# Splitting the first queries' transfer, and reordering the prologue of a one-core attention and expert layer

## Chip, cores and metric

One core of a Trainium2 chip runs one program. The metric is device time in microseconds of one execution; less is better. Times within a trace count from the first instruction.

## What is computed

A transformer layer on x of 2 x 1024 x 128 float32, with 16 heads of 8 columns that share one key and one value head, causal attention, and a routed feed-forward part:

```python
mod = (_silu(L0_c) @ L0_wmod).reshape(L0_c.shape[0], 6, 1, -1)
sa, ca, ga, sb, cb, gb = (mod[:, i] for i in range(6))   # ga, gb: sign kept, magnitude at least 0.25
h = _layernorm(x, axis=-1) * (1 + ca) + sa
x = x + ga * attn(h, w_attn, w_proj)     # q: 16 heads of 8; k, v: one head of 8; softmax over k <= q
h = _layernorm(x, axis=-1) * (1 + cb) + sb
x = x + gb * ffn(h, ...)                 # top 4 of 16 experts by sigmoid gate, plus a shared expert
```

## The kernel before

**Tiling.** The 2048 tokens are 16 units u of 128 tokens and 4 chunks of 512. Chunks are taken in the order `CHUNKS` = 0, 2, 1, 3; c0 is chunk 0 (units 0 to 3 of batch 0), c1 is chunk 2 (units 8 to 11, the start of batch 1). For a unit, two things run on TensorE over its keys: first the maxima (`max` jobs: scores with queries as columns, reduced by VectorE at L768 to one maximum per query and head, 4 jobs for unit 0, 8 for unit 1, 16 for unit 2), then, with the maximum added as two more contraction rows, the `scores` blocks (exponentiated by ScalarE, L628) and the products with the values (`pv`). The maximum of a unit is split into two bfloat16 parts, transposed (`shift`), copied by ScalarE and sent by a transfer into rows 96 and 97 of `qa` (L426).

**Queries and keys.** float32 products are made from bfloat16 parts: a query is split into three parts `qp[0]`, `qp[1]`, `qp[2]` (ScalarE L600, then `q_rest` on VectorE or GpSimd), and six copies of them are stacked in 48 rows of `qa`. `qp` has (feature, head) on its 128 partitions, `qa` has 8 features x 6 products on partitions and heads along the row, so the stacking is six transfers for each chunk (L409), each from 128 partitions of `qp` into 8 partitions of `qa`. Rows 48 to 95 of `qa` are mask marks, sent by `mark` (L376); those of `ka` come once, from `k_marks` (L395). A key chunk is made by `k`, `k_rest`, `k_mid`, `k_set`; a value chunk by `v`. `hT` is the normalized, modulated, transposed input of a chunk, made from `xn` (`norm`), whose statistics are `stats`.

**Order.** One list, `plan`, is written before the program, and every engine walks it in order and does its part of each entry, with semaphores between. The prologue is written out by hand. The rest is made by a loop over the attention blocks: four `scores` steps to a block, each followed by `step`, which advances a clock `now` by 0.87 and emits what is due: maxima by their due steps, and the entries of `side` and `smalls` (each with the time from which it may be emitted). So an entry in `side` with time 2.0 is emitted at the third step. Block n is written scores(n, g), g = 0 to 3. The blocks of unit 0 are n = 0, of unit 1 n = 1, 2, of unit 2 n = 3 to 5, of unit 3 n = 6 to 9.

**Queues.** All transfers that the change touches are issued by SyncE (SP), in the order of the plan, into one queue; SP goes to the next entry as soon as the waits of its own part are met. `fetch` are the expert weights' loads (six issues, L416 to L421). TensorE's `warm` entries are products of the identity with itself whose result nobody reads. The small PSUM bank of `hT`, `k` and later entries is free for the next user when the last one's reader has read it (`small_free`).

Of the kernel before, what the change touches and what calls it, by code (L numbers as in the profile page):

```python
# [5 lines left out]
def adaln_attention_moe_kernel(nc, x_d, w_attn_d, w_proj_d, gate_d, ws_in_d, vs_in_d, ws_out_d,  # L6
# [7 lines left out]
    HD = (w_attn_d.shape[1] - D) // 2  # L14
# [5 lines left out]
    CH = 4 * P  # L20
# [16 lines left out]
    PRODUCTS = ((0, 2), (0, 1), (1, 1), (0, 0), (1, 0), (2, 0))  # L37
# [11 lines left out]
    LAST = CHUNKS[-1]  # L49
# [6 lines left out]
    jobs = []  # L56
    for u in order:
# [4 lines left out]
        w = (t + 1) * P - k0  # L62
# [85 lines left out]
    def one_max():  # L148
        j = st["job"]
        st["job"] += 1  # L150
        plan.append(("max", j))
        if j == last_job[jobs[j][0]]:
            emit(("split_max", jobs[j][0]))
# [26 lines left out]
    def step(cost):  # L180
# [5 lines left out]
    plan += [("stats", c0), ("silu",), ("norm", c0), ("warm", 11), ("cond",), ("warm", 2), ("stats", c1), ("norm", c1)]  # L186
    plan += [("hT", c0), ("warm", 3), ("q", c0), ("q_rest", c0)]
    plan += [("k", c0), ("k_rest", c0), ("k_mid", c0), ("v", c0), ("k_set", c0)]
    side += [(3.0, ("k_set", c1)), (4.0, ("stats", CHUNKS[2])), (6.0, ("stats", CHUNKS[3]))]
    smalls += [(5.0, ("gates",))]  # L190
    side += [(8.0, ("norm", CHUNKS[2])), (90.0, ("norm", CHUNKS[3])), (1.0, ("marks",)), (2.0, ("fetch",)), (20.0, ("w_split", 0)),
             (24.0, ("w_split", 1)), (27.0, ("w_split", 2)), (10.0, ("sentinels",))]

    def through_shift(u):
        while st["job"] <= last_job[u]:
            one_max()
        while ("shift", u) not in plan:
            x = next(x for x in smalls if x[1] == ("shift", u))
            smalls.remove(x)
            emit(x[1])  # L200
# [2 lines left out]
        while st["job"] <= last_job[u]:  # L203
            one_max()

    plan += [("hT", c1), ("q", c1), ("q_rest", c1)]
    max_of(order[0])
    plan += [("k", c1), ("k_rest", c1)]
    max_of(order[1])
    through_shift(order[0])  # L210
    plan += [("k_mid", c1), ("v", c1)]
    for j in range(4):
        one_max()
    through_shift(order[1])
    for n, (u, kt, first, last) in enumerate(blocks):
        if first:
            through_shift(u)
# [57 lines left out]
    with ctx:  # L275
# [3 lines left out]
        def sem(name):  # L279
            return ctx.enter_context(nc.semaphore(name))  # L280
# [65 lines left out]
        x_in = [sem(f"x_in{c}") for c in range(NC)]  # L346
        w_attn_in, w_proj_in, c_in, wmod_in, gate_in = (sem("w_attn_in"), sem("w_proj_in"), sem("c_in"), sem("wmod_in"),
                                                        sem("gate_in"))
        q_in = [sem(f"q_in{c}") for c in range(NC)]
        shift_in = [sem(f"shift_in{u}") for u in range(NU)]  # L350
        consts, wk_ready, rows_ready, cleared = sem("consts"), sem("wk_ready"), sem("rows_ready"), sem("cleared")
# [30 lines left out]
        @block.sync  # L382
        def _(sp):
            xv = x_d.rearrange("b (t p) d -> p (b t) d", p=P)
            sp.dma_start(xs[:, 4 * c0:4 * c0 + 4, :], xv[:, 4 * c0:4 * c0 + 4, :]).then_inc(x_in[c0], 16)
            sp.dma_start(w_attn[:, :], w_attn_d).then_inc(w_attn_in, 16)
            for c in CHUNKS[1:]:
                sp.dma_start(xs[:, 4 * c:4 * c + 4, :], xv[:, 4 * c:4 * c + 4, :]).then_inc(x_in[c], 16)
            sp.dma_start(gate_w[:, :], gate_d).then_inc(gate_in, 16)
            sp.dma_start(w_proj[:, :], w_proj_d).then_inc(w_proj_in, 16)  # L390
            sp.wait_ge(q_marked, 1)
            mark(sp, c0)
            sp.wait_ge(k_marked, 1)
            for b in range(B):
                sp.dma_start(ka[QROWS:QROWS + 64, 1, b, :].rearrange("p (t k) -> p t k", k=P),  # L395
                             k_marks[QROWS:QROWS + 64, :].unsqueeze(1).broadcast_to([64, TB, P])
                             ).then_inc(k_marks_in, 16)
            for x in plan:
                kind = x[0]
                if kind == "q_rest":  # L400
                    c = x[1]
                    b, t0 = c // CB, c % CB * CH
                    sp.wait_ge(q_hi, q_no[c] + 1)
                    for i in range(3):
                        if i == 1:
                            sp.wait_ge(q_parts, q_no[c] + 1)
                        for n in range(len(PRODUCTS)):
                            if PRODUCTS[n][0] == i:
                                sp.dma_start(qa[HD * n:HD * (n + 1), b, :, t0:t0 + CH],  # L409
                                             qp[i][:, q_no[c] % 2, :]).then_inc(q_in[c], 16)  # L410
                elif kind == "marks":
                    for c in CHUNKS[1:]:
                        mark(sp, c)
                elif kind == "fetch":
                    for i, w_d in enumerate((e_win_d, e_vin_d)):
                        sp.dma_start(sl[:, 2 * i:2 * i + 2, :].rearrange("p s (e f) -> p (s e) f", f=F),  # L416
                                     w_d.rearrange("e d f -> d e f")).then_inc(w_in, 16)
                    sp.dma_start(w_out[:, 1:, :], e_wout_d.rearrange("(c s) f d -> (s f) c d", s=EC)).then_inc(w_in, 16)
                    sp.dma_start(sl[:, 4, 0:P], ws_in_d).then_inc(w_in, 16)
                    sp.dma_start(sl[:, 4, P:2 * P], vs_in_d).then_inc(w_in, 16)  # L420
                    sp.dma_start(w_out[:, 0, :], ws_out_d).then_inc(w_in, 16)  # L421
                elif kind == "shift":
                    u = x[1]
                    b, t = u // TB, u % TB
                    sp.wait_ge(small_read[at[x]], use[x] + 1)
                    sp.dma_start(qa[MROWS:SROWS, b, :, t * P:(t + 1) * P], shiftT[:, place[u] % 2, :]  # L426
                                 ).then_inc(shift_in[u], 16)
                elif kind == "combT" and x[1] != LAST:
                    c = x[1]
                    sp.wait_ge(small_read[at[x]], use[x] + 1)  # L430
                    sp.dma_start(comb_d[c], combT[:, :]).then_inc(comb_out[c], 16)
                elif kind == "spread":
                    c = x[1]
                    sp.wait_ge(comb_out[c], 16)
                    if turn_of[c]:
                        sp.wait_ge(gated_up, FC * turn_of[c])
                    rows = comb_d[c].rearrange("(f s) t -> s f t", s=EC)
                    for s in range(EC):
                        sp.dma_start(comb_wide[F * s:F * s + F, :, :],
                                     rows[s].unsqueeze(0).broadcast_to([F, FC, CH])).then_inc(comb_in[c], 16)  # L440
                elif kind == "turn":
                    c = x[1]
                    ov = out_d.rearrange("b (t p) d -> p (b t) d", p=P)
                    sp.wait_ge(small_read[at[x]], use[x] + 1)
                    sp.dma_start(ov[:, 4 * c:4 * c + 4, :], xs[:, 4 * c:4 * c + 4, :]).then_inc(out_sent[c], 16)
            for c in range(NC):
                sp.wait_ge(out_sent[c], 16)

        @block.gpsimd
        def _(gp):  # L450
# [33 lines left out]
            for x in plan:  # L484
                kind = x[0]
                if kind in ("norm", "norm2"):
# [6 lines left out]
                    own(gp.tensor_scalar(rstd[:, us], mv[:, us, 1], EPS, None, ALU.add))  # L493
                    gp.tensor_tensor(rstd[:, us], rstd[:, us], neg_half[:, :], ALU.pow).then_inc(rstd_ready, 1)  # L494
                    k = norm_no[x]
                    if x not in (("norm", c0), ("norm2", LAST)):
                        gp.wait_ge(rstd_ready, k + 1)
                        if k >= 2:
                            before = xn_of[norms[k - 2]]
                            gp.wait_ge(small_ready[at[before]], use[before] + 1)  # L500
                        for i in range(4):
                            u = 4 * c + i
                            ins = gp.tensor_scalar(xn[:, k % 2, i, :], xs[:, u, :], mv[:, u, 0:1], rstd[:, u:u + 1],  # L503
                                                   ALU.subtract, ALU.mult)
                        ins.then_inc(xn_ready, 1)
# [69 lines left out]
        def _(act):  # L575
            act.dma_start(cT[:, :], c_d.rearrange("b d -> d b"), allow_slow_non_contiguous=True).then_inc(c_in, 16)
            act.dma_start(wmod[:, :, :], wmod_d.rearrange("k (j d) -> k j d", j=6)).then_inc(wmod_in, 16)
            for x in plan:
# [15 lines left out]
                elif kind == "q":  # L594
# [2 lines left out]
                    act.wait_ge(small_ready[at[x]], use[x] + 1)  # L597
                    if k >= 2:
                        act.wait_ge(q_in[CHUNKS[k - 2]], len(PRODUCTS) * 16)
                    act.activation(qp[0][:, k % 2, :], small[at[x]][:, :], ACT.Copy).then_inc(q_hi, 1)  # L600
                elif kind == "k":
                    c = x[1]
# [64 lines left out]
        def _(v):  # L667
# [7 lines left out]
            for x in plan:  # L675
                kind = x[0]
                if kind == "stats":
# [6 lines left out]
                    for u in range(4 * c, 4 * c + 4):  # L684
                        ins = v.bn_aggr(mv[:, u, :], stat6[:, u, :])
                    ins.then_inc(stats_ready, 1)
                elif x in (("norm", c0), ("norm2", LAST)):
                    c, k = x[1], norm_no[x]
                    if k >= 2:
                        before = xn_of[norms[k - 2]]  # L690
# [157 lines left out]
        def _(pe):  # L848
# [9 lines left out]
            for x in plan:  # L858
# [43 lines left out]
                elif kind == "max":  # L902
# [3 lines left out]
                    if x[1] == 0 or jobs[x[1] - 1][0] // 4 != u // 4:  # L906
                        pe.wait_ge(k_marks_in, 16 * B)
                        pe.wait_ge(q_marks_in[u // 4], 16)
                        pe.wait_ge(q_in[u // 4], len(PRODUCTS) * 16)
                        pe.wait_ge(k_done, q_no[u // 4] + 1)  # L910
                    if k >= NM:
                        pe.wait_ge(m_read, k - NM + 1)
                    to = m_bank[k % NM][:, 0:n * w].rearrange("p (n w) -> p n w", w=w)
# [143 lines left out]
```

## Time and profile before

| | us |
|---|---|
| median of 3 executions | 440.38 |
| lowest, highest | 437.97, 493.62 |
| the profiled execution | 439.45 |
| its span, first to last instruction | 436.9 |
| TensorE busy in the span | 381.4 |
| VectorE busy | 271.5 |
| ScalarE busy | 222.2 |
| GpSimd busy | 97.0 |

The span is that of the profiled execution; 2.55 us of its time lie around it. Engines are named PE (TensorE), PEld (its weight loads), DVE (VectorE), ACT (ScalarE), POOL (GpSimd), SPq (SyncE issuing transfers). A busy share is an average over stages, so what matters here is read from the first 80 us. TensorE's granted clock has two levels, 1.00 (2.4 GHz) and 0.50 (1.2 GHz); a mean between them is a stretch with both. The share of DMA is that of 16 engines.

### The profile page before, as it was taken

What the parts mean: (1) busy time and instruction counts of PE and PEld (TensorE: products, weight loads), DVE (VectorE), ACT (ScalarE), POOL (GpSimd) and SP (SyncE); (2) the same over time, 40 slices, a digit from 0 to 9 for tenths busy, and PEclk for the clock granted to TensorE, in tenths of its full rate; (3) what the DMA queues carried; (4) which work ended last, traced back from release to release, by engine and by line L of the source; (5) the groups of instructions that cost most, each with busy time, mean ns of one, the idle gap of its engine ahead of it and who ended that gap; (6) DMA issues with size and microseconds to landing.
All of it is one profiled execution on the core that took longest, in us unless ns stands there. A gap on an engine that the chain in (4) does not pass through costs nothing.

```text
span 436.9 us, 5857 instructions
## 1 busy us (share of the span) xinstructions
PE 381.4 (87%) x2065; PEld 178.4 (41%) x2065; DVE 271.5 (62%) x624; ACT 222.2 (51%) x413; POOL 97.0 (22%) x128
## 2 busy tenths in 40 slices
PE   8449879899999986999899999987999998848995
PEld 7235433443463442443554334342534333216542
DVE  4429974898986956794468747865278734113343
ACT  2301437656668642463675545763875446834300
POOL 6511095302300393310260000050046000011000
PEclk9755889999999996999999999996999999995999
DMA  8653951400005300418100000000530000000000
GB/s 209 85 62 49 231 135 27 49 2 2 2 1 137 61 2 0 53 21 173 23 24 3 1 0 26 1 2 0 128 71 2 1 0 26 0 2 0 1 0 24
DMA packets 21851, 17.84 MB, mean 41 GB/s; under 512 B 6656, under 2 KB 18576, under 8 KB 21824
## 3 DMA queue, kind: packets, MB, share of 16 engines
q1 hardware_dynamic: 21408, 17.09, 20.6%
q10 hardware_dynamic: 416, 0.39, 0.3%
q8 instruction: 16, 0.26, 0.3%
q14 instruction: 11, 0.09, 0.1%
HBM read 9.65 MB, written 1.15 MB: 25 GB/s over the span
## 4 chain that ended last, share of the span: by engine, by line
PE 66%; DVE 15%; ACT 6%; POOL 4%; issue 4%; DMA 3%; SPq 1%; POOLq 0%; ACTq 0%; DVEq 0%
PE bank L850 62%; DVE mn L768 9%; DMA qa<-qp 3%; ACT pr L628 2%; POOL xn L503 2%; PE bank L997 2%; POOL rstd L494 1%; ACT L628 1%; PE bank L883 1%; POOL sl L572 1%; SPq L409 1%; ACT fT L663 1%; DVE stat L800 1%; ACT osb L640 1%; ACT hT L592 1%
## 5 line engine op out<-in xcount | busy, mean ns | idle before, releaser
L768 DVE TENSOR_REDUCE mn<-bank 128x1 f32<-128x512 f32 (+3 forms) x304 | 186.5, 655 | 72.6 <-PE bank L850 72.0
L628 ACT ACTIVATE pr<-bank 128x512 f32<-128x512 f32 x288 | 159.3, 598 | 100.2 <-PE bank L850 98.6
L850 PE MATMUL bank<-ka,qa 96*128 96x128 bf16 (+3 forms) x576 | 113.8, 291 | 19.2 <-DVE mn L768 9.8
L850 PE MATMUL bank<-qa,ka 98*128 98x512 bf16 x288 | 109.8, 392 | 4.2 <-DMA qa<-shiftT 2.3
L850 PE MATMUL bank<-pr,va 128*32 128x512 f32 x576 | 80.2, 630 | 0.7 <-ACT pr L628 0.7
L850 PEld LDWEIGHTS bank<-ka,qa 96*128 96x128 bf16 x576 | 51.3, 104 | 68.7 <-DVE mn L768 27.9
L850 PE MATMUL bank<-hT_parts,up_parts 128*128 128x512 f32 x216 | 66.2, 439 | 1.2 <-DVE sl L840 1.1
L850 PEld LDWEIGHTS bank<-qa,ka 98*128 98x128 bf16 x288 | 28.1, 100 | 88.4 <-ACT pr L628 47.7
L850 PEld LDWEIGHTS bank<-hT_parts,up_parts 128*128 128x128 f32 x216 | 40.9, 200 | 18.6 <-issue 6.3
L572 POOL TENSOR_TENSOR sl<-sl,comb_wide 128x512 f32<-128x512 f32 x24 | 29.9, 1278 | 55.1 <-DMA comb_wide<-comb_rows 27.7
L840 DVE TENSOR_TENSOR sl<-sl,bank 128x512 f32<-128x512 f32 x36 | 24.7, 687 | 24.6 <-PE bank L850 19.7
L493 POOL TENSOR_SCALAR rstd<-mv 128x4 f32<-128x4 f32 x8 | 1.9, 233 | 167.9 <-DVE mv L801 167.7
L850 PE MATMUL bank<-sl,w_out 128*128 128x512 f32 x72 | 37.3, 599 | 0.0
L632 ACT ACTIVATE sl<-bank 128x512 f32<-128x512 f32 x36 | 21.4, 599 | 7.8 <-PE bank L850 6.2
L850 PEld LDWEIGHTS bank<-pr,va 128*32 128x32 f32 x576 | 11.5, 109 | 21.6 <-ACT pr L628 11.4
L503 POOL TENSOR_SCALAR xn<-xs,mv,rstd 128x128 f32<-128x128 f32 x24 | 19.4, 820 | 0.6
L640 ACT ACTIVATE osb<-bank 128x512 f32<-128x512 f32 x16 | 9.6, 597 | 16.2 <-PE bank L850 16.2
L592 ACT ACTIVATE hT<-bank,mod 128x512 f32<-128x512 f32 x8 | 6.2, 777 | 22.7 <-PE bank L883 22.7
L789 DVE RECIPROCAL rec<-bank 128x16 f32<-128x16 f32 x16 | 4.0, 252 | 20.0 <-PE bank L997 19.9
L997 PE MATMUL bank<-ident,osb 128*128 128x128 f32 x64 | 9.9, 277 | 6.6 <-ACT fT L663 3.8
L850 PEld LDWEIGHTS bank<-sl,w_out 128*128 128x128 f32 x72 | 13.0, 190 | 4.7 <-DVE sl L840 0.8
L663 ACT ACTIVATE fT<-bank,gs 128x512 f32<-128x512 f32 x4 | 2.8, 688 | 22.9 <-PE bank L850 22.9
(128 smaller groups left out, 257.8 us busy)
## 6 DMA issues: line engine op xcount, KB each, us to landing
comb_wide<-comb_rows SPq DMA_DIRECT2D x6, 1024.0 KB, 9.9
qa<-q_marks SPq DMA_DIRECT2D x4, 768.0 KB, 8.8
qa<-qp SPq DMA_DIRECT2D x24, 128.0 KB
xs<-in_L_attn_x SPq DMA_DIRECT2D x4, 256.0 KB, 5.3
out_x<-xs SPq DMA_DIRECT2D x4, 256.0 KB, 2.3
sl<-in_L_ffn_e_win SPq DMA_DIRECT2D x1, 512.0 KB, 11.0
sl<-in_L_ffn_e_vin SPq DMA_DIRECT2D x1, 512.0 KB, 10.6
w_out<-in_L_ffn_e_wout SPq DMA_DIRECT2D x1, 512.0 KB, 5.1
```

The costliest lines, as they stand in the source:

```text
L409: sp.dma_start(qa[HD * n:HD * (n + 1), b, :, t0:t0 + CH], qp[i][:, q_no[c] % 2, :]).then_inc(q_in[c], 16)
L503: ins = gp.tensor_scalar(xn[:, k % 2, i, :], xs[:, u, :], mv[:, u, 0:1], rstd[:, u:u + 1], ALU.subtract, ALU.mult)
L572: gp.tensor_tensor(sl[:, f, :], sl[:, f, :], comb_wide[:, f - 1, :], ALU.mult).then_inc(gated_up, 1)
L592: act.activation(hT[:, c, :], small[at[x]][:, :], ACT.Identity, scale=mod[:, j + 1, b:b + 1], bias=mod[:, j, b:b + 1]).then_inc(small_read ...
L628: act.activation(pr[:, n % NPB, g, :], s_bank[in_s[x] % NS][:, :], ACT.Exp, scale=SCALE).then_inc(s_read, 1)
L632: act.activation(sl[:, f, :], s_bank[in_s[x] % NS][:, :], ACT.Silu).then_inc(s_read, 1)
L640: act.activation(osb[:, p % 2, :], o_bank[:, :], ACT.Copy).then_inc(evac_done, 1)
L663: act.activation(fT[:, :], small[at[d]][:, :], ACT.Copy, scale=gs[:, 0, c // CB:c // CB + 1]).then_inc(small_read[at[d]], 1)
L768: v.tensor_reduce(mn[:, place[u] % 2, part, h:h + n], m_bank[k % NM][:, 0:n * w].rearrange("p (n w) -> p n w", w=w), AX.X, ALU.max, negate ...
L840: v.tensor_tensor(sl[:, f, :], sl[:, f, :], m_bank[k % NM][:, :], ALU.mult).then_inc(m_read, 1)
L850: return pe.matmul(out, lhsT, rhs, start=start, stop=stop, skip_group_check=True)
L997: ins = pe.transpose(small[at[x]][:, i * P:(i + 1) * P], osb[:, place[u] % 2, i * P:(i + 1) * P], ident[:, :])
```

## The change

In the prologue: GpSimd no longer normalizes c1, VectorE does. c1's keys and values are prepared before the first maximum instead of among the maxima, and 24 warm-up products stand before the first maximum. The c0 queries go in twelve transfers of half the tokens: six for tokens 0 to 255, then six for tokens 256 to 511 with a semaphore of their own (`q_in_rest`), on which TensorE waits at the first maximum of unit 2. The loads of the chunks 1 and 3 of x, of gate_w and of w_proj are issued after c1's queries instead of at the start. The marks of the chunks 2, 1, 3 are issued at plan times 4, 44 and 60 instead of all three at 1; the fetch at 13 instead of 2; the weights' splits on GpSimd at 34, 38, 41 instead of 20, 24, 27.

```diff
-    side += [(3.0, ("k_set", c1)), (4.0, ("stats", CHUNKS[2])), (6.0, ("stats", CHUNKS[3]))]
+    side += [(4.0, ("stats", CHUNKS[2])), (6.0, ("stats", CHUNKS[3]))]
...
-    side += [(8.0, ("norm", CHUNKS[2])), (90.0, ("norm", CHUNKS[3])), (1.0, ("marks",)), (2.0, ("fetch",)), (20.0, ("w_split", 0)),
-             (24.0, ("w_split", 1)), (27.0, ("w_split", 2)), (10.0, ("sentinels",))]
+    side += [(8.0, ("norm", CHUNKS[2])), (90.0, ("norm", CHUNKS[3])), (4.0, ("marks", c1)), (13.0, ("fetch",)), (34.0, ("w_split", 0)),
+             (38.0, ("w_split", 1)), (41.0, ("w_split", 2)), (44.0, ("marks", CHUNKS[2])), (60.0, ("marks", CHUNKS[3])), (10.0, ("sentinels",))]
...
-    plan += [("hT", c1), ("q", c1), ("q_rest", c1)]
+    plan += [("hT", c1), ("q", c1), ("q_rest", c1), ("k", c1), ("k_rest", c1), ("k_mid", c1), ("v", c1), ("k_set", c1)]
+    plan += [("loads",), ("warm", 24)]
     max_of(order[0])
-    plan += [("k", c1), ("k_rest", c1)]
     max_of(order[1])
-    through_shift(order[0])
-    plan += [("k_mid", c1), ("v", c1)]
-    for j in range(4):
-        one_max()
-    through_shift(order[1])
...
-            for c in CHUNKS[1:]:
+            for c in CHUNKS[1:2]:
                 sp.dma_start(xs[:, 4 * c:4 * c + 4, :], xv[:, 4 * c:4 * c + 4, :]).then_inc(x_in[c], 16)
-            sp.dma_start(gate_w[:, :], gate_d).then_inc(gate_in, 16)
-            sp.dma_start(w_proj[:, :], w_proj_d).then_inc(w_proj_in, 16)
...
+                    for s0, w in ((0, CH // 2), (CH // 2, CH // 2)) if c == c0 else ((0, CH),):
+                        for i in range(3):
+                            if i == 1 and s0 == 0:
+                                sp.wait_ge(q_parts, q_no[c] + 1)
+                            for n in range(len(PRODUCTS)):
+                                if PRODUCTS[n][0] == i:
+                                    sp.dma_start(qa[HD * n:HD * (n + 1), b, :, t0 + s0:t0 + s0 + w],
+                                                 qp[i][:, q_no[c] % 2, s0:s0 + w]).then_inc(q_in_rest if s0 else q_in[c], 16)
+                elif kind == "loads":
+                    for c in CHUNKS[2:]:
+                        sp.dma_start(xs[:, 4 * c:4 * c + 4, :], xv[:, 4 * c:4 * c + 4, :]).then_inc(x_in[c], 16)
+                    sp.dma_start(gate_w[:, :], gate_d).then_inc(gate_in, 16)
+                    sp.dma_start(w_proj[:, :], w_proj_d).then_inc(w_proj_in, 16)
                 elif kind == "marks":
-                    for c in CHUNKS[1:]:
-                        mark(sp, c)
+                    mark(sp, x[1])
...
-                elif x in (("norm", c0), ("norm2", LAST)):
+                elif x in (("norm", c0), ("norm", c1), ("norm2", LAST)):
...
+                    if u == 4 * c0 + 2 and jobs[x[1] - 1][0] != u:
+                        pe.wait_ge(q_in_rest, len(PRODUCTS) * 16)
```

## Rows read from the trace of the kernel before

**Rows 1.** The page: TensorE's busy time, and its granted clock in 40 slices.

```profile
PE 381.4 (87%) x2065; PEld 178.4 (41%) x2065; DVE 271.5 (62%) x624; ACT 222.2 (51%) x413; POOL 97.0 (22%) x128
...
PEclk9755889999999996999999999996999999995999
```

**Rows 2.** Chain of waits, first 60 us: start, us, what.

```profile
15.59 12.09 DMA qa<-qp
...
58.21 2.07 DMA qa<-shiftT
```

**Rows 3.** Timeline of PE, first 42 us: start, length, line, operation, [idle before].

```profile
1.87 5.06 PE L850 MATMUL bank<-ident 128*128 128x128 f32 x22 [1.87 <-POOL ident L468]
...
9.24 0.83 PE L850 MATMUL bank<-ident 128*128 128x128 f32 x6
...
12.87 1.06 PE L850 MATMUL bank<-w_attn,hT 128*128 128x8 f32 x8 [0.56 <-DVE q_left L733]
16.39 0.66 PE L883 MATMUL bank<-ident,xn 128*128 128x128 f32 x4 [2.46 <-POOL xn L503]
17.97 2.08 PE L850 MATMUL bank<-hT,wq 128*128 128x512 f32 x2 [0.93 <-ACT hT L592]
...
27.93 1.98 PE L850 MATMUL bank<-ka,qa 96*128 96x128 bf16 x16 [7.88 <-DMA qa<-qp]
...
40.55 0.61 PE L850 MATMUL bank<-qa,ka 98*128 98x512 bf16 x1
```

**Rows 4.** Table of windows: stretch, busy by engine, PE clock, DMA share, GB/s.

```profile
13.50:27.50 14.00, 3.16 (x10) 1.26 (x10) 3.33 (x7) 2.10 (x3) 4.60 (x6) 0.63 0.57 65
28.00:40.00 12.00, 11.09 (x66) 7.59 (x67) 10.29 (x20) 1.57 (x3) 1.16 (x1) 0.50 0.51 55
40.60:41.60 1.00, 1.00 (x7) 0.60 (x7) 0.72 (x3) 0.67 (x2) 0.00 (x0) 0.50 0.00 0
```

**Rows 5.** DMA view: 4 to 44 us in 1-us slices; packets from 38 to 40.

```profile
GB/s 357 347 321 297 192 208 208 198 137 59 110 56 65 53 69 51 72 51 72 51 70 53 66 56 58 62 69 70 53 70 53 69 53 67 39 1 0 0 19 231
...
DMA packets 66, 0.04 MB, mean 20 GB/s; under 512 B 42, under 2 KB 65, under 8 KB 65
```

**Rows 6.** Timeline of SP's issues: start, length, what.

```profile
37.43 4.17 SPq L426 DMA_DIRECT2D qa<-shiftT  x2
...
45.16 2.33 SPq L416 DMA_DIRECT2D sl<-in_L_ffn_e_win  x1
47.54 6.69 SPq L416 DMA_DIRECT2D sl<-in_L_ffn_e_vin  x1
```

**Rows 7.** Table of windows where attention begins.

```profile
41.52:59.21 17.69, 14.85 (x86) 6.77 (x84) 17.46 (x49) 7.45 (x15) 4.25 (x5) 0.82 0.95 226
...
60.33:65.48 5.15, 5.15 (x28) 2.42 (x29) 3.87 (x9) 2.39 (x5) 4.90 (x11) 0.67 0.01 5
65.48:69.02 3.54, 2.95 (x23) 1.26 (x21) 0.69 (x1) 2.86 (x7) 2.92 (x2) 1.00 0.00 1
```

**Rows 8.** Timeline of DVE and POOL in the prologue.

```profile
7.51 1.18 DVE L695 TENSOR_SCALAR xn<-xs,mv,rstd 128x128 f32<-128x128 f32 x4 [0.98 <-POOL rstd L494]
...
11.51 1.04 POOL L494 TENSOR_TENSOR rstd<-rstd,neg_half 128x4 f32<-128x4 f32 x1
...
12.13 0.69 DVE L733 TENSOR_TENSOR q_left<-bank,qp 128x512 f32<-128x512 f32 x1 [1.56 <-ACT qp L600]
...
12.66 3.67 POOL L503 TENSOR_SCALAR xn<-xs,mv,rstd 128x128 f32<-128x128 f32 x4
```

**Rows 9.** Timeline of DVE, 33 to 49 us: the maxima's reductions and k_set.

```profile
33.15 4.87 DVE L768 TENSOR_REDUCE mn<-bank 128x2 f32<-128x512 f32 x8
...
39.30 1.94 DVE L768 TENSOR_REDUCE mn<-bank 128x1 f32<-128x384 f32 x4
...
41.52 5.85 DVE L768 TENSOR_REDUCE mn<-bank 128x1 f32<-128x384 f32 x12 [0.28 <-PE bank L850]
...
48.90 0.28 DVE L754 COPY ka<-k_all 98x512 bf16<-98x512 bf16 x1
```

More of the change, by code:

```diff
@@ L348, in adaln_attention_moe_kernel @@
                                                         sem("gate_in"))
+        q_in_rest = sem("q_in_rest")
         q_in = [sem(f"q_in{c}") for c in range(NC)]
@@ L403, in _ @@
                     sp.wait_ge(q_hi, q_no[c] + 1)
[L404 to L410, printed above, removed]
+                    for s0, w in ((0, CH // 2), (CH // 2, CH // 2)) if c == c0 else ((0, CH),):
[11 more added lines that the diff above has]
+                    sp.dma_start(w_proj[:, :], w_proj_d).then_inc(w_proj_in, 16)
                 elif kind == "marks":
-                    for c in CHUNKS[1:]:
-                        mark(sp, c)
+                    mark(sp, x[1])
                 elif kind == "fetch":
@@ L495, in _ @@
                     k = norm_no[x]
-                    if x not in (("norm", c0), ("norm2", LAST)):
+                    if x not in (("norm", c0), ("norm", c1), ("norm2", LAST)):
                         gp.wait_ge(rstd_ready, k + 1)
@@ L599, in _ @@
                         act.wait_ge(q_in[CHUNKS[k - 2]], len(PRODUCTS) * 16)
+                        act.wait_ge(q_in_rest, len(PRODUCTS) * 16)
                     act.activation(qp[0][:, k % 2, :], small[at[x]][:, :], ACT.Copy).then_inc(q_hi, 1)
```

## Prediction

> **What bounds the kernel now.** I read the page first. PE is busy 87% of the span [rows 1], so after the start-up the kernel is a PE stream; what the change touches is the time before and just after that stream begins. The chain of waits, read for the first 60 us, shows the reader the two places where PE stands still for data: 12.09 us of it are the transfer qa<-qp, ending at 27.7, and 2.07 us are qa<-shiftT, ending at 60.3 [rows 2]. The PE timeline says the same from PE's side: the first maxima start at 27.93 after 7.88 us of idleness, and the first scores block runs at 40.55 [rows 3].
>
> Next the table of windows, for the DMA. While the twelve qa<-qp transfers of the first two chunks drain (13.5 to 40), the queue moves only 55 to 65 GB/s with about half of the 16 engines busy, and stays at that rate after PE, DVE and ACT have fallen idle [rows 4]. Each moves 128 x 512 x 2 B = 131 KB, so all twelve are 1.57 MB; at 60 GB/s that is 26.2 us, 2.18 us each. From 38 to 40 only 66 packets are left to start, most of them the small ones of shiftT; at 40.6 the queue is empty [rows 4, 5]. So the first scores at 40.55 start just as the queue runs dry: shift(0)'s transfer was issued at 37.43 [rows 6] behind the second chunk's queries in the same queue.
>
> From 28 on, DVE is the engine without slack: 17.46 us busy of 17.69 between 41.52 and 59.21 [rows 7]. TensorE's granted clock is at the lower level (0.50, 1.2 GHz) in the slices from 17 to 48 us, after it had done little since 14 [rows 1, 3], but DVE's reductions set the pace, so this costs little. PE waits at 58.2 because SP was issuing the expert weights' loads (one issue of 6.69 us behind three marks); shift(2)'s issue comes after them at 58.21 [rows 2]. That stall is followed by half clock (0.67 mean), and the block from 60.33 takes 5.15 us where the next takes 3.54 [rows 7].
>
> **The change, part by part.**
>
> *Loads out of the prologue.* 2 x 256 KB of x, gate_w and w_proj leave the queue ahead of the marks. The first q transfers start their packets about 1.2 us after issue, with only the tail of k_marks beside them; I give this 0.3 us and no more.
>
> *Norm of the second chunk on DVE.* It takes 1.18 us there (the first chunk's row) instead of 3.67 on POOL [rows 8]. But it stands ahead of q_rest(c0) on DVE and waits for rstd: 11.51 + 1.04 = 12.55, so it ends at 13.75 and q_rest(c0), at 12.13 before [rows 8], starts 1.6 us later; q_parts comes at 15.8 instead of 14.1. k_rest(c0) ends at 16.6, which frees the PSUM bank for hT(c1) only then: the transposes start at 16.65 where they started at 16.39 [rows 3]. The faster norm buys nothing, since the bank is late next. ACT does k_mid(c0) first, then hT(c1) to 18.2; q(c1) takes 2.08 us at half clock [rows 3], to 20.3.
>
> *Second chunk's k and v ahead of the maxima.* k(c1) 20.3 to 22.4, v(c1) 22.4 to 24.2 (twice the 1.06 us of v(c0) [rows 3], less overlap). The steps behind them (POOL's split of q, k_rest, k_mid, POOL's subtraction, k_set), each under 2 us and one after another, end near 26.6, in front of the first maximum on DVE and earlier than PE comes to it.
>
> *24 warm-up products.* 22 matmul records took 5.06 us at the start and 6 took 0.83 at full clock [rows 3], so one product (two records) costs 0.45 us or 0.25. [...] If full clock held all along, 27.2; if it stayed half, 34.5. They are in PE's own order ahead of the first maximum.
>
> *Queries in two halves.* Six halves of 65.5 KB at 60 GB/s are 1.09 us each: three from 13.3 to 16.6, a gap to 17.0 (the late q_parts, SP issue and 1.2 us), the rest to 20.3, landed near 21 instead of 27.7. No engine uses these 6.5 us, for PE reaches the first maximum at 31.2, later than its 27.93. Bounds of a half, which no row shows: 1.09 us (bytes decide) and 2.18 (each transfer costs what a whole one does). Packets of 512 B ran at up to 357 GB/s in the loads [rows 5], so they are not slow as such; I take 1.09.
>
> *What comes first after that.* The queue holds 12 halves and 6 wholes, the same 26.2 us plus the 0.4 gap less 0.3: last packets start at 39.1 as before. Then come the moved loads, 520 KB in front of shift(0): on the engines that carried the queries some 73 packets of 512 B, about 2.0 us at 350/16 GB/s [rows 5]. shift(0) follows, so the first scores start near 40.5 + 1.9 = 42.4. DVE is ready: twelve maxima at 0.60 us (4.87 us less one duration, over 7 [rows 9]) from 31.9 end at 39.2. Cover of 3.2 us; it is gone only if the warm-ups stay slow.
>
> *The first steps of attention.* At 42.95 DVE begins job 12, where before it began job 16 at 41.52 [rows 9]: 1.43 later, plus four more reductions of 1.94 together, less the two copies of k_set already done (0.45 on the path, the first is 0.28 [rows 9]), less 0.2 of idleness: +2.7. PE, kept to DVE's pace, arrives at scores(3,0) at 57.8 + 2.7 = 60.5 rather than leaving it at 60.33: +0.2.
>
> *Marks and fetch later.* SP meets shift(2) before the fetch, so the 2.28 us stall is not repeated; nothing on SP but shift(1), one mark and shift(2) stands before it. The remaining marks are issued when SP reaches them, at least four steps ahead of the maxima that want them (4 x 0.9 us against a transfer of 3.6 us plus issue): hidden, with at most 1 us in doubt. shift(3) stands behind a fetch of some 8.4 us (2.33 twice [rows 6] and the four shorter issues behind them), issued from about 52, done 60.5, and is needed near 72: hidden. The block after 60.5 keeps the full clock: 3.54 rather than 5.15, of which DVE, 3.87 us busy in that block [rows 7], takes back 0.2: -1.4.
>
> Sum: +0.2 - 1.4 = -1.2 us. The profiled execution took 439.45 us (span 436.9 and 2.55 around it), 0.2% under the median of 440.38. 439.45 - 1.2 = 438.2.
>
> What the pages say of the transfer. The window shows 65 GB/s [rows 4] into eight partitions. The Trainium skill (SBUF — State Buffer, section on the DMA port swizzle) has bandwidth depend on how many ports the partitions reach; eight partitions from a multiple of eight reach two of its 27.2 GB/s ports, 54 GB/s. By that the twelve take an estimated 29 us rather than 26, and a half is half. The Trainium skill (DMA: Bandwidth & Descriptors, Anatomy of one DMA) speaks against the change: about 2.0 us fixed per transfer plus bytes over 436 GB/s. Strictly one after another that is 2.3 us a whole, close to the row, and 2.15 a half.
>
> **The rivals.**
> *A, a half costs as much as a whole (slower).* Place: qa<-qp's twelve halves. For: 2.18 us per transfer would look the same. Against: about half the engines are busy without a break [rows 4], which pure waiting would not show. The queue is then 12 x 1.09 = 13 us longer, the first scores start at 55.3, and the kernel takes 438.2 + 12.9 = 451. Anything above 1.19 us a half makes it slower than before, above 1.9 by 2%. 0.10 for all of it, 0.09 for a part (442 to 448).
> *B, the halves overlap into different destinations and drain faster.* For: two neighbours write to different partitions. Against: twelve wholes did not [rows 4]. DVE's 39.2 and the shift's issue then bind: PE transposes at 37.7, issue 38.3, 2.07 us [rows 2], scores at 40.3: 436. 0.07.
> *C, the clock rises late or not at all in the warm-ups.* Maxima from 34.5, shift(0) issued at 41.4, scores at 43.5: 439.3. For: it stayed low for 30 us before. 0.08.
> *D, the early half is worth its whole time.* First maxima 6.5 us sooner and everything behind them, plus 2.3 and 1.6: 429. It needs PE free at 21 and the queue empty; rows 3 and 4 are against both. 0.06.
>
> **Numbers.** Forecast 0.60 (435.5 to 441.5), A 0.19, B 0.07, C 0.08, D 0.06. Full A and D lie outside the range; 434 to 445 also leaves out about 0.04 of partial A. About 2% (8.8 us) is what a measurement of this kernel tells from no change: faster is D, 0.06; slower is full A and the top of its part, 0.10; within, 0.84.
>
> **What would show it.** Right: first maximum near 31, not 21; first scores at 41.5 to 43.5, just as the queue is dry; q transfers at about 60 GB/s with no change of rate between halves and wholes; no wait for shiftT near 60 and no half clock behind it; scores(4,0) near 64.2 (65.48 before). Wrong: a drain that ends near 52 (A), scores that start before 41 (B or D), a new wait of PE for q_marks, or a half-clock stretch in a new place, each of which is worth 1 to 2 us.

## Result and profile after

The changed kernel takes 449.07 us (median of 4, 448.26 to 450.2) against 439.18 for the kernel before (median of 4). The ratio is 1.0256, with a 95% interval of 1.0177 to 1.0334: it is slower, and whether by more than 2% is not clear. The difference of the medians is 9.9 us; against the 63 executions of the kernel before that ran beside the experiments (medians 440.07 to 441.21) it is 8 to 9 us. The forecast was 438.2. Medians here are of all executions, but the ratios leave out those that took over 1.5% more than the fastest of the same kernel: one of the kernel before, four of the ten of experiment 1's first kernel, two of the twelve of experiment 6's second.

The page of the changed kernel, its slices of TensorE's granted clock (span 446.5 us, 11.2 us a slice):

```profile
PE   8695989969999995999899998987999998956996
...
PEclk9775596997999999799999999997799999995999
```

Beside the clock line before [rows 1] the low stretch of the prologue reaches through the fifth slice (to 56 us), a longer one than before stands in the seventh slice (67 to 78 us; before, in the sixth), and there is one more in the tenth (100 to 112). Behind 110 us the two traces run in parallel, 10.1 us apart, to the last scores block. So the whole loss is made before 110.

PE's timeline of the changed kernel, from the warm-ups to the first scores (start, length, line, operation, [idle before]):

```profile
25.73 5.05 PE L850 MATMUL bank<-ident 128*128 128x128 f32 x37
30.61 0.83 PE L850 MATMUL bank<-ka,qa 96*128 96x128 bf16 x12
31.79 0.40 PE L850 MATMUL bank<-ka,qa 96*128 96x128 bf16 x4 [0.34 <-DVE mn L768]
...
41.92 0.61 PE L850 MATMUL bank<-qa,ka 98*128 98x512 bf16 x1 [4.11 <-DMA qa<-shiftT]
42.33 5.39 PE L850 MATMUL bank<-ka,qa 96*128 96x256 bf16 x24
47.51 0.63 PE L850 MATMUL bank<-qa,ka 98*128 98x512 bf16 x1
```

The first maximum starts at 30.61 (27.93 before [rows 3]) directly behind the warm-ups, though the first half of the queries had landed at 21.16. PE then waits 4.11 us for shift(0)'s transfer, which stands in the queue behind c1's queries (the last landed at 40.42) and the loads. The first scores start at 41.92 (40.55 before), the second step at 47.51 (44.29 before): twelve reductions between them where there were eight.

The table of windows of the changed kernel (stretch and its length; busy time of PE, PEld, DVE, ACT, POOL; PE clock, DMA share, GB/s):

```profile
13.50:25.30 11.80, 8.96 (x33) 6.35 (x34) 5.39 (x12) 3.50 (x5) 2.01 (x3) 0.65 0.54 67
...
52.52:57.80 5.28, 5.28 (x22) 2.30 (x21) 5.09 (x23) 1.52 (x4) 0.03 (x1) 0.50 0.87 196
62.19:68.55 6.36, 4.22 (x31) 2.01 (x29) 4.54 (x11) 3.25 (x7) 5.62 (x12) 0.98 0.09 27
68.55:74.06 5.51, 5.34 (x23) 1.94 (x22) 0.69 (x1) 2.96 (x6) 0.00 (x0) 0.50 0.01 1
...
95.39:105.56 10.17, 7.28 (x37) 3.54 (x35) 7.20 (x16) 2.67 (x6) 5.33 (x5) 0.68 0.01 2
```

The first line answers [rows 4]: halves of a transfer drain at 67 GB/s where whole ones drained at 65. The second and fourth are stretches at 0.50 in which PE is busy throughout or nearly so; the last one is the block that took 5.20 us in the trace before and takes 10.17 now. The stall of [rows 2] at 58 is gone, but there are other waits. PE's three largest waits from 27 to 130 (in total, times, longest):

```profile
PE bank L850 <- DVE mn L768: 4.9, 9, 2.0
PE bank L850 <- DMA qa<-shiftT: 4.1, 1, 4.1
PE bank L883 <- POOL xn L502: 2.1, 1, 2.1
```

Block starts, scores(n, 0), in the profiled executions, as PE's timeline has them (us, and the difference to before):

| block | before | changed | marks and fetch later, alone (exp. 4) | splits later, alone (exp. 1) | all put right (exp. 9) |
|---|---|---|---|---|---|
| 0 | 40.55 | 41.92 (+1.4) | 40.99 (+0.4) | 40.49 (-0.1) | 40.27 (-0.3) |
| 3 | 60.33 | 62.19 (+1.9) | 58.85 (-1.5) | 60.97 (+0.6) | 58.23 (-2.1) |
| 4 | 65.48 | 68.55 (+3.1) | 66.09 (+0.6) | 67.73 (+2.2) | 62.22 (-3.3) |
| 5 | 69.02 | 74.06 (+5.0) | 71.55 (+2.5) | 71.30 (+2.3) | 65.94 (-3.1) |
| 10 | 90.27 | 95.39 (+5.1) | 92.80 (+2.5) | 92.55 (+2.3) | 87.19 (-3.1) |
| 12 | 99.25 | 109.46 (+10.2) | 101.77 (+2.5) | 106.12 (+6.9) | 97.70 (-1.5) |

So there are two losses: 5 us up to block 5, and 5 us between blocks 10 and 12.

One caution for the table: each column is one execution, and executions of one kernel differ by some us. Near 300 us, for example, the trace before has two stretches at 0.50 (3.4 and 6.8 us), and the traces of experiments 1 (first kernel), 4 and 9 (second kernel) have one (3.4 us); each of the three gains 2.7 us there, and no edit touches that part. So the medians of the executions decide, and the table only says where the time goes.

### The profile page after: what moved, and what is told of

It is laid out like the page before. It is cut to its first block, busy times and chain, and to the rows that moved or that the text cites. A ratio compares the mean times of both kernels' runs of the same rounds, so it can differ in the third digit from the quotient of the medians.

```text
span 446.5 us, 5960 instructions
## 1 busy us (share of the span) xinstructions
PE 394.9 (88%) x2113; PEld 186.9 (42%) x2113; DVE 272.9 (61%) x628; ACT 222.8 (50%) x413; POOL 93.2 (21%) x124
## 4 chain that ended last, share of the span: by engine, by line
PE 64%; DVE 17%; POOL 8%; ACT 5%; issue 4%; DMA 1%; POOLq 0%; ACTq 0%; DVEq 0%
PE bank L850 60%; DVE mn L768 10%; POOL xn L502 3%; ACT pr L628 2%; POOL rstd L493 2%; PE bank L999 1%; PE bank L883 1%; ACT L628 1%; DMA qa<-shiftT 1%; POOL sl L571 1%; DVE xn L695 1%; ACT fT L663 1%; DVE stat L800 1%; ACT hT L591 1%; PE bank L929 0%
## 5 line engine op out<-in xcount | busy, mean ns | idle before, releaser
L850 PE MATMUL bank<-qa,ka 98*128 98x512 bf16 x288 | 112.0, 400 | 6.2 <-DMA qa<-shiftT 4.1
L850 PE MATMUL bank<-pr,va 128*32 128x512 f32 x576 | 81.9, 643 | 0.7 <-ACT pr L628 0.7
L850 PEld LDWEIGHTS bank<-ka,qa 96*128 96x128 bf16 x576 | 50.3, 102 | 62.2 <-DVE mn L768 30.6
L850 PE MATMUL bank<-ident 128*128 128x128 f32 x80 | 14.1, 353 | 1.9 <-POOL ident L467 1.9
L502 POOL TENSOR_SCALAR xn<-xs,mv,rstd 128x128 f32<-128x128 f32 x20 | 15.6, 795 | 0.5
```

Of the source, the lines that this page charges most:

```text
L850: return pe.matmul(out, lhsT, rhs, start=start, stop=stop, skip_group_check=True)
```

## Experiments

The kernel before ran beside each group of kernels; its medians there were 440.78, 440.07 and 441.21 us. The ratios are each group's own, so two kernels of different groups are compared by their medians. Theory at the start: late splits (S) made the second loss; in the first, the moved loads and chunk 1's norm share it, and the halves and warm-ups do nothing.

### 1. The weights' splits on GpSimd

On the changed kernel:

```diff
-(34.0, ("w_split", 0)), (38.0, ("w_split", 1)), (41.0, ("w_split", 2))
+(20.0, ("w_split", 0)), (24.0, ("w_split", 1)), (27.0, ("w_split", 2))
```

> The changed kernel with the weights' splits on GpSimd back at plan times 20, 24, 27. Theory S (late splits meet chunk 1's key copies on VectorE and hold them): the two copies take 0.28 us each again instead of 1.88 and 1.12, PE's wait of 2.05 us near 98 and the half-clock stretch from 99 to 106 are gone, time about 449 - 5 = 444. Rival (the 10 us come from the start-up alone, the later stretch would come anyway): 449, the stretch stays.

Measured: 443.8 us (median of ten, 438.23 to 446.34; 441.5 for the six that the ratio uses), ratio to before 1.003 (0.9991 to 1.007). The second loss is gone: blocks 5 and 12 are both 5.0 us late. So 5.3 us come back, or 7.6 by the six. And the other way round, the same edit alone on the kernel before:

> The kernel before with only the weights' splits on GpSimd moved to plan times 34, 38, 41. Theory S (collision with chunk 1's key copies on VectorE): the copies L754 and L755 of chunk 1 grow from 0.28 us to over 1 each, PE waits about 2 us for VectorE near 93, half clock follows, the time is 439 + 5 = 444. Rival (the collision needs the changed kernel's prologue): 439, no such wait.

Measured: 444.89 us, ratio 1.0101 (1.0048 to 1.0154); of the 6.9 us at block 12 in its trace, 4.6 arise between blocks 10 and 12. Its other 2.3 us stand before any split, and the windows say where they come from: behind the same stall for shiftT (2.37 us here, 2.28 in the trace before) the clock stayed at 0.50 for 6.8 us, not 3.4. First the kernel before, then this one:

```profile
61.70:64.90 3.20, 3.20 (x16) 1.07 (x15) 3.06 (x8) 0.93 (x3) 3.14 (x6) 0.50 0.02 5
61.10:67.70 6.60, 6.60 (x28) 3.12 (x27) 3.65 (x9) 2.88 (x5) 3.76 (x9) 0.50 0.01 4
```

What happens between blocks 10 and 12, in the changed kernel's timelines of DVE and of POOL (start, length):

```profile
94.54 1.88 DVE L754 COPY ka<-k_all 98x512 bf16<-98x512 bf16 x1
96.34 1.12 DVE L755 COPY ka<-k_all 48x512 bf16<-48x512 bf16 x1
...
93.92 2.35 POOL L459 TENSOR_TENSOR up_parts<-sl,up_parts 128x1024 fp32r<-128x1024 f32 x1
96.22 1.10 POOL L458 CAST up_parts<-sl 128x1024 fp32r<-128x1024 f32 x1
```

and with the splits early (experiment 1's first kernel), the same copies on DVE and the last split on POOL, and then the same in the kernel before:

```profile
94.44 0.28 DVE L754 COPY ka<-k_all 98x512 bf16<-98x512 bf16 x1
94.64 0.28 DVE L755 COPY ka<-k_all 48x512 bf16<-48x512 bf16 x1
...
83.58 0.73 POOL L459 TENSOR_TENSOR up_parts<-sl,up_parts 128x256 fp32r<-128x256 f32 x1
```

```profile
89.42 0.28 DVE L754 COPY ka<-k_all 98x512 bf16<-98x512 bf16 x1
...
78.55 0.73 POOL L460 TENSOR_TENSOR up_parts<-sl,up_parts 128x256 fp32r<-128x256 f32 x1
```

The reader should add start and length. The first copy ends at 96.42, 0.15 us behind the end of GpSimd's product (93.92 + 2.35 = 96.27); the second at 97.46, 0.14 behind the end of the cast (97.32). Alone each copy takes 0.28 us; here each ended just behind the GpSimd instruction that had started before it. The kernel with only the late splits shows the same two lengths, 1.88 and 1.12. The maxima behind them came late, PE waited 2.05 and 0.84 us, and then the clock was at 0.50 from 99 to 106: 2.9 us of waiting for DVE and the low clock behind it make the 5. The Trainium skill (SBUF — State Buffer, section on the two separate sides) has it that VectorE in its two-port modes and GpSimd take a shared port pair exclusively, for a whole instruction. The ends of both copies agree with that; that the copies ran in such a mode no run here shows.

### 2. The halved transfer

The first chunk's queries in six whole transfers again, without the second semaphore:

```diff
-for s0, w in ((0, CH // 2), (CH // 2, CH // 2)) if c == c0 else ((0, CH),):
+for s0, w in ((0, CH),):
```

> The changed kernel with the first chunk's queries in six whole transfers again, on one semaphore. Theory (the early half is not used, since the first maximum stands behind the second chunk's work and 24 warm-ups until 30.6, and bytes set the drain): the queries land near 27.6, first maximum still near 30.6, first scores near 41.9, time within 1 us of the changed kernel. Rival D (the early half is worth time): first maximum or first scores later, 451 or more.

Measured: 449.17 us, ratio to before 1.0231 (1.0168 to 1.0294), beside 449.07 for the changed kernel. First maximum at 30.66, first scores at 41.62, block 12 at 9.9 us behind before. The halves are worth nothing here and cost nothing.

### 3. The loads

x, gate_w and w_proj loaded at the start again:

```diff
-            for c in CHUNKS[1:2]:
+            for c in CHUNKS[1:]:
...
-    plan += [("loads",), ("warm", 24)]
+    plan += [("warm", 24)]
```

> The changed kernel with the loads of x, gate_w and w_proj issued at the start again. Theory (shift(0)'s transfer stands in one queue behind the queries and these loads): first scores about 1.4 us sooner, near 40.5, time 1 to 2 us less than the changed kernel if VectorE's backlog carries it on, about 447.5. Rival (loads are hidden, or hurt the first queries more): first scores unchanged near 41.9, time the same.

Measured: 445.88 us, ratio 1.0137 (1.0094 to 1.0179): 3.2 us less than the changed kernel. The first scores start at 38.81, not 41.92. PE's row in this kernel:

```profile
38.81 0.61 PE L847 MATMUL bank<-qa,ka 98*128 98x512 bf16 x1 [3.73 <-DMA qa<-shiftT]
```

Even so it waits for the queue. Of the 3.1 us, 2.9 are still there at block 12 (+7.3 instead of +10.2). They are not all the loads' doing. In this execution c1's queries had themselves landed at 38.97, 1.4 us sooner than in the changed kernel; with the same prologue they landed at 40.29 in experiment 7, and at 40.41 in experiment 9, which has four maxima more, and the first scores started at 40.49 and 40.27. What repeats is the distance from the last of c1's queries to shift(0): 1.4 to 1.6 us in five traces with the loads late (changed; experiments 1, 2, 5 and 6), about 0.2 or less, either way, in the three with the loads first. So the loads in front of shift(0) are worth about 1.5 us at the first scores, and why the medians differ by 3.2 is in part open.

### 4. Marks and fetch alone

On the kernel before, only `marks` at 4, 44, 60 and `fetch` at 13:

> The kernel before with only the marks spread to 4, 44, 60 and the fetch at 13. If the wait for shiftT near 60 were worth what the prediction booked (2.3 us and 1.6 of half clock): 439 - 3.5 = 435.5. Rival (the chain behind it is late next: GpSimd's gates and norm of chunk 1, which start from VectorE's work and not from PE's): PE waits at the transposes of hT for most of the gain, and the time is 438 to 439.

Measured: 442.25 us, ratio 1.0017 (0.9982 to 1.0052): no gain, as the rival has it. The stall for shiftT is gone and block 3 starts 1.5 us sooner, but PE's timeline goes on so:

```profile
62.59 0.39 PE L849 MATMUL bank<-qa,ka 98*128 98x512 bf16 x1
65.19 1.12 PE L882 MATMUL bank<-ident,xn 128*128 128x128 f32 x4 [2.20 <-POOL xn L502]
66.09 1.06 PE L849 MATMUL bank<-qa,ka 98*128 98x512 bf16 x2
```

PE arrives earlier at the transposes of chunk 1, GpSimd's xn does not come earlier, and the wait moves by one block with its size (2.28 to 2.20). The low clock moves with it, too, and lasts 6.8 us in this execution, 3.4 in the trace before.

That xn is late next could be read before the change. Its chain starts with VectorE's copy of the gates and ends with GpSimd's norm 10.6 us later; PE's transposes need it. The kernel before, then the changed one:

```profile
54.11 0.41 DVE L723 COPY sl<-bank 128x256 f32<-128x256 f32 x1
61.57 3.14 POOL L503 TENSOR_SCALAR xn<-xs,mv,rstd 128x128 f32<-128x128 f32 x4
65.03 0.61 PE L883 MATMUL bank<-ident,xn 128*128 128x128 f32 x4
...
57.26 0.41 DVE L723 COPY sl<-bank 128x256 f32<-128x256 f32 x1
64.72 3.13 POOL L502 TENSOR_SCALAR xn<-xs,mv,rstd 128x128 f32<-128x128 f32 x4
67.92 0.84 PE L883 MATMUL bank<-ident,xn 128*128 128x128 f32 x4 [2.13 <-POOL xn L502]
```

In the kernel before xn is ready at 64.71 and PE, held up by the stall, comes at 65.03. So without the stall block 4 could start 0.3 us sooner and no more, as long as GpSimd's chain stays where it is.

### 5. The warm-ups

The changed kernel without `("warm", 24)`:

> The changed kernel without the 24 warm-up products. Theory (the first scores wait for the queue, not for PE): first maximum on PE near 24 and VectorE's first reduction near 27 instead of 31, first scores unchanged near 42, time that of the changed kernel, 449, within 1 us. Rival (warm-ups are on the path): first scores and the end some 3 us sooner, 446. Other rival (warm-ups buy the clock and are needed): later than 450.

Measured: 449.87 us, ratio 1.0192 (1.0125 to 1.0258), beside 449.07 for the changed kernel: no difference that stands out of the noise. The maxima run early and PE then waits more than twice as long for the same transfer:

```profile
23.36 1.44 PE L850 MATMUL bank<-ka,qa 96*128 96x128 bf16 x12
...
42.51 0.61 PE L850 MATMUL bank<-qa,ka 98*128 98x512 bf16 x1 [8.96 <-DMA qa<-shiftT]
```

### 6. Chunk 1's norm ahead of the gates

On the changed kernel, with the transposes left where they stood:

```diff
-(8.0, ("norm", CHUNKS[2]))
+(4.5, ("norm", CHUNKS[2]))
-            smalls.append((now + 4.0, ("hT", a)))
+            smalls.append((now + (8.0 if a == CHUNKS[2] else 4.0), ("hT", a)))
```

> The changed kernel with chunk 1's norm ahead of the gates on GpSimd (plan time 4.5 instead of 8), its transposes left in their place. Theory (the wait of 2.13 us for xn near 68 and the half clock from 68 to 75 are a third separate loss): no wait for xn, no half-clock stretch near 70, block 6 about 4 us sooner than 77.7, time 449 - 4 = 445; the stretch near 99 stays. Rival (the wait only moves, to w_projg or to the queries of chunk 1): 448 to 449.

Measured: 446.44 us, ratio 1.0085 (1.0043 to 1.0128). The wait for xn is gone, but the gates, now second on GpSimd, are what PE waits for:

```profile
65.21 0.49 PE L850 MATMUL bank<-w_projg,yT 128*128 128x128 f32 x2 [2.22 <-POOL w_projg L527]
```

Block 4 is no earlier (68.97); block 5 is 1.5 us earlier (72.56). The low stretch near 70 is 3.4 us long here and 6.8 in the changed kernel's trace, but the edit need not be the reason: in experiment 1's first kernel, where the norm stands as in the changed kernel, it is 3.4 too. The rival was half right: 2.6 us by the medians and 1.5 by the block starts, not 4. The same reorder with the spread on the kernel before:

> The kernel before with marks and fetch spread as in the change, and chunk 1's norm ahead of the gates on GpSimd (plan time 4.5 instead of 8), its transposes left where they stood in the plan. Theory (norm on GpSimd is late next when the shiftT stall goes): PE no longer waits for xn near 65 and keeps the full clock there; scores(4,0) near 62 (65.48 before, 66.1 with the spread alone), time 3 to 4 us under before, 436. Rival (something else stands right behind, or the clock falls anyway): scores(4,0) at 65 or later, time as before.

Measured: 439.87 us, ratio 0.9968 (0.9933 to 1.0003): no more than a hint, where the theory had 436. Its profiled execution took 443.9 us and was late already in the prologue (first scores at 43.73), so I read nothing from its trace.

### 7. Three put right together

The changed kernel with the splits early, the loads first and the norm ahead of the gates:

> The changed kernel with three things taken back or moved: weights' splits at 20, 24, 27; loads at the start; chunk 1's norm ahead of the gates. Theory (these three are the whole of the loss): 449 - 5 (splits) - 3 (loads) - 4.6 (wait for xn and the half clock behind it) = 436.5. Rival (the prologue's order, which puts four maxima fewer ahead of the first scores, costs too): 440 or more.

Measured: 438.73 us, ratio 0.996 (0.9928 to 0.9993). The three together give back about 10 us, the whole of the loss, though the theory had 436.5. Block 12 is 0.5 us behind before. Two of the three take a part of the change back. The third, the norm ahead of the gates, is not in the kernel before either, so the fair partner is the second kernel of experiment 6 (0.9968, in the same group): it has the same spread and the same norm, and the old prologue. Beside it, all that is left of the change (norm on VectorE, c1's keys and values first, four maxima fewer ahead of the first scores, halves, warm-ups) makes no measurable difference, 0.996 against 0.9968.

### 8. Four maxima ahead of the first scores

```diff
     max_of(order[0])
     max_of(order[1])
+    through_shift(order[0])
+    for j in range(4):
+        one_max()
+    through_shift(order[1])
```

> The changed kernel with four maxima of unit 2 and the second shift put ahead of the first scores, as the kernel before had them. Theory (VectorE idles from 39.2 until the queue is dry at 42, and these four would fit there): second scores step near 45.6 instead of 47.5; the end 1 to 2 us sooner if that is carried on, 447.5. Rival (it only shifts idleness, since chunk 1's xn is next): the steps to block 3 sooner, blocks from 6 on within 0.5 us of the changed kernel.

Measured: 448.61 us, ratio 1.0148 (1.0096 to 1.02). In its trace the queue ran dry later than in the other kernels with the changed prologue (first scores at 43.40, theirs at 42.67 or before), and the second step was still at 47.13, 3.73 us behind instead of 5.59. At block 5 it is 1.3 us ahead of the changed kernel, and the low clock (0.50 from 96.2 to 109.8) takes this back by block 12. Inconclusive: the medians differ by 0.5 us, the ratio suggests a gain, and the trace does not hold it to the end.

### 9. A version better than both

First on the kernel before: marks and fetch spread, gates at plan time 1 instead of 5, chunk 1's norm at 5.5 instead of 8, its transposes 7 instead of 4 behind it and so left about in their place, so that GpSimd has both ready:

> The kernel before with marks and fetch spread, the gates at plan time 1 instead of 5 and chunk 1's norm at 5.5 instead of 8, its transposes in their place. Theory (with the shiftT stall gone and both of GpSimd's products ready in time nothing is late next): PE waits for neither w_projg nor xn, no half clock between 55 and 160, scores(4,0) near 62 instead of 65.5, time 436, ratio 0.991. Rival (the clock or VectorE takes it back): ratio 0.996 to 1.000.

Measured: 437.98 us, ratio 0.9944 (0.9915 to 0.9974): faster, by 0.6% where the theory had 0.9%. Block 4 started at 64.09 (the theory had 62), and from block 4 to block 20 PE does not wait for GpSimd and there is no low clock. Then the changed kernel with all that was found (not shown: the loads at the start as in experiment 3, the transposes as just above):

```diff
-(5.0, ("gates",))
+(1.0, ("gates",))
-(8.0, ("norm", CHUNKS[2]))
+(5.5, ("norm", CHUNKS[2]))
-(34.0, ("w_split", 0)), (38.0, ("w_split", 1)), (41.0, ("w_split", 2))
+(20.0, ("w_split", 0)), (24.0, ("w_split", 1)), (27.0, ("w_split", 2))
...
-    plan += [("loads",), ("warm", 24)]
+    plan += [("warm", 24)]
     max_of(order[0])
     max_of(order[1])
+    through_shift(order[0])
+    for j in range(4):
+        one_max()
+    through_shift(order[1])
```

> The changed kernel with the weights' splits at 20, 24, 27, the loads at the start, the gates at 1 and chunk 1's norm at 5.5, and the four maxima and the second shift ahead of the first scores. What is left of the change is the halved transfer, the second chunk's preparation ahead of the maxima on VectorE, the warm-ups, and marks and fetch spread. Theory: as the kernel before with the same spread, or 1 us later for the warm-ups' time: 436 to 437. Rival (the prologue's order is a loss of its own): 439 or more.

Measured: 434.56 us (433.27 to 437.77), ratio 0.9859 (0.9817 to 0.9902), about 6 us under before and better than the 436 to 437 expected. Its trace is 3.1 us ahead at block 5, but only 1.5 at block 12, behind a low stretch from 91.3 to 94.7, and gains 2.7 near 300 us, where no edit is. So where all of the 6 us come from is not shown. PE's waits from 27 to 130 in this kernel, to be laid beside those of the changed kernel:

```profile
PE bank L851 <- DVE mn L769: 3.6, 11, 0.8
PE bank L851 <- DMA qa<-shiftT: 1.6, 1, 1.6
```

and its table of windows for blocks 3 and 4:

```profile
58.23:62.22 3.99, 3.81 (x31) 1.90 (x28) 3.89 (x10) 2.69 (x7) 3.01 (x2) 1.00 0.03 9
62.22:65.94 3.72, 2.95 (x23) 1.26 (x21) 1.89 (x4) 3.02 (x8) 0.39 (x1) 1.00 0.01 1
```

Block 3 takes 3.99 us at full clock, 5.15 before. This is the gain that the prediction had booked for the spread alone (1.2 us of its 1.4), and it comes only once GpSimd's two products are ready.

## Where the prediction was right and where it failed

*Right, in the prologue.* Norm on DVE ended at 13.67 (forecast 13.75), transposes at 16.47 (16.65), v(c1) in 1.79, first maximum 30.61 (31.2), first half landed at 21.16 (21), first scores 41.92 (42.4). A half costs half (67 GB/s), so rival A falls. Neither figure that the prediction takes from the Trainium skill fits: the rate is above 54 GB/s, and a half at 67 GB/s takes 1.0 us, not 2.15. The section that the prediction names has the 2.0 us fixed for transfers that GpSimd issues, and SyncE issues these. First maximum after 30 fells D; the clock rose during the warm-ups (1.00 from 27.3 to 34.1), which fells C; scores at 41.92 fell B. The early half is unused, as said, and experiments 2 and 5 show that neither halves nor warm-ups are on the path. The queue was dry when forecast (c1's queries landed at 40.42, forecast near 40.5), and the loads took 1.5 us behind them where 1.9 was allowed.

*Sums that do not hold, without effect on the outcome.* No row of the kernel before shows the 31.2 taken for the first maximum; the run showed 30.61. The lower bound beside it, 27.2, is wrong: 24 products at 0.25 us from 24.2 on end at 30.2. The loads are 584 KB, not 520; by the rate used, 73 packets are 1.7 us, not 2.0.

*Failed, the first steps of attention: "+0.2".* I took PE as kept to DVE's pace. The granted clock fell at 34, after PE had worked 0.40 us in every 0.60 under DVE's pace (the rows at 31.79), and stayed at 0.50 to 58, ten microseconds longer than before. Between 52.52 and 57.80 PE was busy 5.28 us of 5.28 at that level, and DVE 5.09: there PE was the bound, if by little. Block 3 started at 62.19 instead of 60.5. No run takes this clock by itself away, so its share of the 1.7 us is argued and not shown.

*Failed, "The block after 60.5 keeps the full clock ...: -1.4".* This step took a wait away and did not ask who is late next on GpSimd. The gates and the norm of chunk 1 follow DVE's copy of the gates (54.11 before, 57.26 now), so the +2.7 that the forecast itself had for DVE held for them too: xn came 3.1 us later while PE was only 0.8 later at the end of block 3. PE waited 2.13 us for it, the clock was low from 68 to 75, and blocks 3 and 4 lost 3 us (+1.9 to +5.0) instead of winning 1.4. Experiment 4 shows the same on the kernel before: without its stall, the wait stands one block on.

*Failed, an edit left without a price.* The sum has no term for the splits at 34, 38, 41. In the kernel before, GpSimd was idle while the copies ran (its last split ended at 79.3, the copies stood at 89.42); the change laid 8 us of GpSimd work over them. That is 5 us of the 10, shown by experiment 1 in both directions. "A half-clock stretch in a new place, ... worth 1 to 2 us" was named as a danger; there were two, and with the waits that opened them they cost 3 and 5.

The share of each, by medians beside the changed kernel's 449.1: splits 5.3 us, loads 3.2, norm ahead of the gates 2.6; all three together 10.3, against the 11.1 of their sum. The first and third come from ten executions each that spread over 8 and 6 us, so each share is good to a microsecond or two.

What stays open: how much four maxima ahead of the first scores are worth by themselves; where the second half of the loads' 3.2 us goes; and how long the clock stays low behind a wait. Behind one wait of PE of 1.3 to 2.4 us between 58 and 69 us it was not low at all (experiment 7), low for 3.4 us (before; the first kernels of experiments 1 and 6; experiment 8) or for 6.8 us (changed; experiments 2, 3, 4 and 5; the second kernel of experiment 1). So one trace does not give the price of a wait.

## What to carry to other kernels

When an edit removes a stall, list what each engine that was not stalled delivers next and when; the gain ends at the first of these that is late. Work moved on an idle GpSimd was not free here, since VectorE copies ran beside it; so price it at the place it goes to, not at the place it leaves. A transfer that arrives sooner is worth nothing while its reader stands behind other entries of its own queue.

## What was not expected of the hardware

A VectorE copy of 0.28 us took 1.88 us under one GpSimd instruction of 2.35 us and ended 0.15 us behind it. From 42.33 to 57.80 PE was busy 15.46 us of 15.47, as the profile counts it, and the clock stayed at 0.50 all the time. Twelve transfers of 65 KB, each into eight partitions, drained at 67 GB/s where whole ones of 131 KB drained at 65, so the 512-byte pieces lost nothing here. SP's issue of gate_w took 4.16 us behind two loads of x, in a queue still full of queries:

```profile
25.36 2.79 SPq L408 DMA_DIRECT2D xs<-in_L_attn_x  x2
28.19 4.16 SPq L409 DMA_DIRECT2D gate_w<-in_L_ffn_gate_w  x1
32.40 0.43 SPq L410 DMA_DIRECT2D w_proj<-in_L_attn_w_proj  x1
```
